# New slots for the steps of an attention and expert kernel on four engine queues

## What is computed

```
# 1: group norm (4 channels a group), attention over all 1024 positions
h = group_norm(x) * gn_scale + gn_bias
w = softmax((h wq + bq)(h wk + bk)^T * 64**-0.5)
x = x + (w (h wv + bv)) wo + bo
# 2: layer norm, causal attention
n = layer_norm(x);  x = x + softmax(causal(n Wq^T (n Wk^T)^T / 8)) (n Wv^T)
# 3: layer norm, experts that choose tokens (32 experts, 8 tokens each, per image)
u = layer_norm(x);  p = softmax(u gate_w^T + gate_b, over the 1024 positions)
topv, topi = the 8 largest of p per image and expert
pooled[b, e] = sum over k of topv * u[topi]
o[b, e] = gelu([pooled, 1] weight1[e]); o = [o, 1] weight2[e]
x = x + scatter_add(topi, topv * o)
```

## Time and profile before

| | |
|---|---|
| median of three runs | 1200.07 us (1199.62 to 1205.99) |
| the profiled execution | 1198.53 us, span 1196.8 us |
| mean granted TensorE clock | 0.845 |
| busy VectorE / ScalarE / GpSimd | 586.5 / 464.6 / 418.9 us |
| DMA | 47.53 MB, mean 40 GB/s |

### The profile page before, as it was taken

One profiled execution on the slowest core, in us unless ns is written; L12 is line 12 of the kernel. 1 busy time (PEld: TensorE's weight loads), 2 busy tenths in 40 slices (PEclk: granted clock), 3 DMA queues, 4 the chain that ended last, 5 costly groups with the idle time before them and its releaser, 6 DMA issues. The chain is left out here.

```text
span 1196.8 us, 14532 instructions
## 1 busy us (share of the span) xinstructions
PE 920.4 (77%) x4278; PEld 527.1 (44%) x4278; DVE 586.5 (49%) x1663; ACT 464.6 (39%) x952; POOL 418.9 (35%) x246
## 2 busy tenths in 40 slices
PE   2777888787888787887878887878878788866546
PEld 1334454534444453535444454545453444434326
DVE  3544554445564554544455544545454545544124
ACT  2222444353535343443435343434435353442320
POOL 1162524262616244242626152442426261610000
PEclk9985978798898888797988888897879888876758
DMA  4010011020201111010202011111102011000089
GB/s 89 11 43 27 18 27 36 5 58 9 58 10 45 23 27 40 27 40 1 57 9 57 9 45 22 26 40 27 31 9 57 9 31 36 23 18 23 18 177 268
DMA packets 67368, 47.53 MB, mean 40 GB/s; under 512 B 36047, under 2 KB 56815, under 8 KB 67311
## 3 DMA queue, kind: packets, MB, share of 16 engines
q1 hardware_dynamic: 67311, 46.90, 16.2%
HBM read 27.88 MB, written 10.49 MB: 32 GB/s over the span
## 5 line engine op out<-in xcount | busy, mean ns | idle before, releaser
L883 ACT ACTIVATE probs<-scores 128x512 f32<-128x512 f32 (+3 forms) x496 | 252.8, 514 | 455.9 <-PE scores L741 450.2
L1121 DVE TENSOR_REDUCE maxima<-maxima_in 128x1 f32<-128x512 f32 (+3 forms) x496 | 276.8, 581 | 271.9 <-PE maxima_in L720 268.0
L970 POOL TENSOR_TENSOR prob_sum<-prob_sum,probs 128x1024 f32<-128x1024 f32 x96 | 227.0, 2365 | 58.4 <-ACT probs L883 54.5
L720 PE MATMUL maxima_in<-keys,queries 128*128 128x512 f32 (+3 forms) x496 | 210.4, 453 | 27.8 <-DVE maxima L1121 27.3
L741 PE MATMUL scores<-queries,keys 128*128 128x512 f32 (+3 forms) x496 | 196.6, 397 | 0.0
L720 PEld LDWEIGHTS maxima_in<-keys,queries 128*128 128x128 f32 x496 | 108.7, 220 | 105.4 <-DVE maxima L1121 72.0
L739 PE MATMUL scores<-queries_lo,keys_hi 65*128 65x512 f32 x256 | 128.4, 502 | 34.2 <-DMA queries_lo<-rows 31.4
L759 PE MATMUL values_out<-probs,x_sb 128*64 128x512 f32 x512 | 144.7, 692 | 1.0 <-ACT probs L883 1.0
L937 POOL TENSOR_TENSOR ln<-ln,minus_half 128x8 f32<-128x8 f32 x32 | 52.8, 1649 | 251.5 <-DVE ln L1106 251.5
L947 POOL TENSOR_TENSOR x_stack<-x_twice,x_stack 64x1024 fp32r<-64x1024 f32 x16 | 37.4, 2339 | 229.9 <-ACT x_stack L819 229.9
L741 PEld LDWEIGHTS scores<-queries,keys 128*128 128x128 f32 x496 | 108.4, 218 | 8.2 <-issue 3.4
(11 more groups left out here) (174 smaller groups left out, 1107.6 us busy)
## 6 DMA issues: line engine op xcount, KB each, us to landing
x_twice<-in_x_t SPq DMA_DIRECT2D x32, 256.0 KB, 4.1
x_halves<-in_x_t SPq DMA_DIRECT2D x16, 256.0 KB, 2.7
x_sb<-in_x SPq DMA_DIRECT2D x16, 256.0 KB, 3.0
keys_hi<-keys SPq DMA_DIRECT2D x16, 256.0 KB, 3.0
u_all<-u_sb SPq DMA_DIRECT2D x16, 256.0 KB, 2.6
t_scratch<-t SPq DMA_DIRECT2D x16, 256.0 KB, 3.0
total<-t_scratch SPq DMA_DIRECT2D x16, 256.0 KB, 4.9
w_sb<-in_w SPq DMA_DIRECT2D x1, 2080.0 KB
```

Source lines behind the costliest of these rows:

```text
L720: pe.matmul(maxima_in[:, p % NM, 0:w * P], queries[s][q][:, c * P:(c + 1) * P], keys[s][q][:, h * HALF:h * HALF + w * P], start=not diagon ...
L883: nc.scalar.activation(probs[:, t % NP, lo:hi], scores[:, (u + (s - 1) * len(UNITS_1)) % NST, 0:hi - lo], ACT.Exp, scale=SCALE).then_inc(e ...
L970: nc.gpsimd.tensor_tensor(prob_sum[:, :], prob_sum[:, :], new, ALU.add).then_inc(rows_added, 1)
L1121: V.reduce_max(maxima[s][:, c, h:h + 1], maxima_in[:, p % NM, 0:w * P], AX.X).then_inc(maxima_taken, 1)
```

## The change

Only the tables of slots change. No instruction is added, removed or altered, and the semaphores keep their order.

```diff
 AT = {
-    "pe": {"f2.out": 2, "p1.qa": 6, "p1.qb": 11, "p1.ka": 16, "p1.kb": 22, "moe.tr": 24, "moe.lg": 26, "r2": 29,
-           "f1.rs": 3, "f1.out": 5, "p1.g1": 7, "p1.g2": 9, "p1.w": 12, "p2.tr": 15, "p2.qa": 19, "p2.qb": 22,
-           "r1": 26},
-    "act": {"p1.qa": 7, "p1.qb": 12, "l2b": 14, "p1.ka": 17, "l2c": 18, "p1.kb": 23, "moe.tr": 25, "moe.lg": 27,
-            "p1.g1": 8, "p1.w": 13, "p2.tr": 15, "p2.qa": 19, "p2.qb": 22, "xp": 24},
-    "dve": {"f2.out": 2, "l2a": 4, "p1.qa": 8, "p1.qb": 13, "p1.ka": 18, "p1.kb": 24, "r2": 28,
-            "p1.st": 1, "f1.rs": 3, "f1.out": 5, "l1a": 6, "p1.g1": 7, "p1.g2": 9, "p1.g3": 11, "p1.w": 13,
-            "p2.tr": 16, "p2.qa": 20, "p2.qb": 23, "r1": 25},
-    "pool": {"l2a": 6, "l1a": 7, "l1b": 8, "p1.g2": 10, "xp": 25},
+    "pe": {"f1.rs": 2, "f1.out": 4, "p1.g1": 1, "p1.g2": 3, "p1.w": 9, "p2.tr": 20, "p2.qa": 27, "p2.qb": 29,
+           "r1": 26, "p1.qa": 6, "p1.qb": 14, "p1.ka": 16, "p1.kb": 22, "r2": 27, "f2.out": 6, "moe.tr": 23,
+           "moe.lg": 24},
+    "act": {"p1.g1": 0, "p1.w": 9, "p2.tr": 20, "p2.qa": 27, "p2.qb": 29, "xp": 22, "p1.qa": 6, "p1.qb": 12,
+            "p1.ka": 16, "p1.kb": 18, "l2b": 17, "l2c": 17, "moe.tr": 18, "moe.lg": 23},
+    "dve": {"p1.st": 0, "f1.rs": 3, "f1.out": 9, "l1a": 9, "p1.g1": 1, "p1.g2": 3, "p1.g3": 6, "p1.w": 10,
+            "p2.tr": 21, "p2.qa": 22, "p2.qb": 29, "r1": 21, "p1.qa": 7, "p1.qb": 14, "p1.ka": 20, "p1.kb": 26,
+            "r2": 29, "f2.out": 0, "l2a": 8},
+    "pool": {"l1a": 20, "l1b": 29, "p1.g2": 11, "xp": 29, "l2a": 17},
 }
 AT_FIRST = {
-    "pe": {"p1.g1": 1, "p1.g2": 2, "p1.w": 4},
+    "pe": {"p1.g1": 1, "p1.g2": 2, "p1.w": 4, "p1.qa": 6, "p1.qb": 11, "p1.ka": 16, "p1.kb": 22},
...
 PIECE_SLOTS = {
-    1: [1, 3, 5, 7, 9, 11, 12, 13, 14, 15, 16, 17, 19, 21, 23],
-    2: [2, 3, 4, 6, 7, 8, 9, 10, 11, 12, 14, 16, 17, 19, 20, 22],
+    1: [7, 7, 11, 15, 17, 17, 18, 19, 21, 21, 23, 23, 24, 24, 26],
+    2: [0, 0, 1, 2, 4, 11, 13, 14, 15, 17, 17, 18, 19, 20, 21, 21],
 }
-VALUE_SLOTS = {1: [9, 17, 25, 1], 2: [9, 17, 24, 1]}
-ADD_SLOTS = [None, 4, 8, 12, 16, 20, 24, 1]
-COPY_SLOT = {1: 2, 2: 2}
-BIAS_SLOT = 6
+VALUE_SLOTS = {1: [15, 27, 28, 1], 2: [10, 22, 29, 0]}
+ADD_SLOTS = [None, 10, 21, 22, 25, 27, 29, 11]
+COPY_SLOT = {1: 0, 2: 1}
+BIAS_SLOT = 12
```

More of the change, by code:

```diff
@@ L63 @@
 AT = {
[9 rows of a table removed]
+    "pe": {"f1.rs": 2, "f1.out": 4, "p1.g1": 1, "p1.g2": 3, "p1.w": 9, "p2.tr": 20, "p2.qa": 27, "p2.qb": 29,
+           "r1": 26, "p1.qa": 6, "p1.qb": 14, "p1.ka": 16, "p1.kb": 22, "r2": 27, "f2.out": 6, "moe.tr": 23,
+           "moe.lg": 24},
[6 rows of a table added]
 }
 AT_FIRST = {
-    "pe": {"p1.g1": 1, "p1.g2": 2, "p1.w": 4},
-    "act": {"p1.g1": 1, "p1.w": 4},
-    "dve": {"p1.st": 0, "p1.g1": 1, "p1.g2": 2, "p1.g3": 3, "p1.w": 4},
[4 rows of a table added]
     "pool": {"p1.g2": 2},
```

## The result

The changed kernel takes 911.9 us (905.89 to 913.72, four runs) where the kernel before took 1202.9 (1199.62 to 1205.99) beside it: a ratio of 0.757, interval 0.753 to 0.762. Its profiled execution took 911.55 us, with a span of 909.8.

The account below looks back on a forecast made before the run. TensorE's waits and the clock falls behind them were taken as the bound: 65.15 = 46.2 + 6.4 + 12.5 us per iteration. Iterations at 49.8 and the edges gain 219 from 1198.5; 979.5, with 1.5 for the median 981 us, range 925 to 1005.

Parts of the forecast that it names:

- ScalarE holds no score: Rival: late exponentials on ScalarE hold TensorE's scores; 52.8 us per iteration, 1023 us in all, chance 0.14.
- f1.rs waits for a sum: Sign of being wrong: second half, f1.rs waits for GpSimd's sums; forecast had them at 2.5 us, f1.rs at 4.0.
- the two with a slow clock: Rivals: clock falls remain in two stretches, 1052 us, chance 0.13; or whole second half at half clock, 1274, 0.08.
- better than 925, with pieces that keep up: Outcome below the forecast range, with VectorE's maxima pieces not delaying TensorE; under 925 us, chance 0.04.
- the clock rival: Rival: short second-half waits still lower TensorE's clock; 54.9 us per iteration, 1052 us in all, chance 0.13.
- 46.2 + 3.65 = 49.8 per iteration: Each loop iteration: TensorE's 46.2 us of work at full clock plus 3.65 of new waits, where it took 65.1.
- p1.ka for p1.qb's low part: First half: TensorE's p1.ka waits 0 to 0.8 us for VectorE's low part of p1.qb, taken as 0.4.
- The row of r2: Second half's first score waits for the row a DMA brings after r2: 0.5 us left of 2.70.
- The pieces: Second half, f1.out to r1: TensorE waits for the piece two before, seven times 0.15 to 0.4, 1.9 us.
- r1: 0.4 taken: End of VectorE's unbroken stretch in the second half: TensorE waits 0.4 us at r1.
- p2.qb: 0.15 taken: Second half: p2.qb waits for p2.qa's copy and subtraction, 0.15 us left of 0.91.
- The 0.8 for the meeting with the bias: First half: VectorE's first l2a addition meets GpSimd's running bias and loses 0.8 us, between nothing and 1.5.

Follow-up runs that it names:

- short_reduce: Changed kernel, but each maxima piece of the second half is reduced over 256 of its 512 columns on VectorE; 894.5 us.
- undo_p1w: Changed kernel with p1.st, p1.g1, p1.g2, p1.g3 and p1.w back at their old slots on TensorE, ScalarE and VectorE; 976.6 us.
- bias_late: Changed kernel with GpSimd's bias addition moved from slot 12 to 18, behind l2a's power; 913.4 us.
- gate_behind: Changed kernel, but in iteration 15's second half VectorE does the first expert gate behind f1.out and l1a, not ahead; 917.0 us.

## Why the prediction was wrong

**The direction and the causes were right.** The waits of f2.out, r2, p1.w and both rows went; the granted clock of an iteration rose from 0.87 to 1.00, and TensorE's busy time fell from 52.63 to 45.55, where 46.2 was expected at full clock. VectorE runs from f1.out to r1 with one pause. ScalarE holds no score, and f1.rs waits for a sum in iteration 15 alone (0.91): those two rivals fell, and so did the two with a slow clock. The time lies where the prediction had put 0.04 ("better than 925, with pieces that keep up"); but the pieces do not quite keep up, by `short_reduce`. Beside the clock rival stood the Trainium skill (TensorE: Matmul & The Clock Gate, "A second HAM failure mode: psum-queue depth-cycling"); the runs bear it out in part. Up to three waits of 0.75 to 1.16 us an iteration left the clock at 1.00 in nearly all iterations; four of 0.90 to 0.97 (`undo_p1w`) brought the lower level in eight of thirteen.

**The step that failed is the sum "46.2 + 3.65 = 49.8 per iteration"; it measures 46.15.** It adds numbers read with two rulers. The 3.65 of new waits came from a walk by starts, in which a matmul of 512 columns takes 0.23 to 0.34 until the next can start. The 46.2 came from busy time, in which the same matmul lasts 0.40 to 0.50, since its modelled end lies behind the next start. After a wait, the first part of the wait lies inside that tail and is called busy. The two pieces at 502.04 take 1.10 us together, 0.40 more than the first pair in `short_reduce`, and only 0.10 of it shows as idle time (each is shown busy for 0.50, and they start 0.60 apart). The second one alone:

```profile
502.64 0.51 PE L722 MATMUL maxima_in<-keys,queries 128*128 128x512 f32 x1
```

So what was added as waits was in part counted as work already. `short_reduce` bounds the true split. Its iteration takes 45.2, and by starts its r1 still waits 0.54 of that (0.65 behind the score at 498.17, for 0.11 between two such scores, 509.71 and 509.82). So TensorE's own work is at most 44.7 and waits are at least 1.45 in the changed kernel. The base was too high by at least 1.5, the waits by the rest of the 3.65, at most 2.2; over 13 iterations 47 us, over the 14th 3.6.

**Its single waits, by starts.** p1.ka for p1.qb's low part: 0.4 taken; p1.ka starts at 476.57, 0.24 behind the matmul ahead, as without a wait: nothing. The row of r2: 0.5 taken; the first score starts 0.24 behind the one ahead too (489.38, 489.62): nothing. The pieces: 1.9 taken, 0.9 to 1.1 found by taking VectorE's work away. r1: 0.4 taken; it starts 0.38 behind the score at 509.82, for 0.11 without a wait: 0.27, up to the negation. p2.qb: 0.15 taken; its operand lands at 512.50, just behind the end of the value group ahead (512.47), and that fits. So the mechanism was right at the pieces, r1 and p2.qb, with sizes too large; two of the waits were not there.

**The lock.** l2a was put at 2.8 us and takes 2.86 (472.82 to 475.68). The 0.8 for the meeting with the bias stood on VectorE's side, with the bias running first; in the trace VectorE's addition starts 0.16 ahead of the bias, and the bias on GpSimd paid 0.45. The addition's 0.75 (0.68 in the earlier trace rows) is not the bias's doing, since it takes 0.76 in `bias_late` too: it starts 0.20 ahead of the end of GpSimd's add (from 470.63 on, 2.39 us). In iteration 15 it starts 0.76 ahead of that end and takes 1.31:

```profile
746.97 2.39 POOL L969 TENSOR_TENSOR prob_sum<-probs 128x1024 f32<-128x1024 f32 x1 [11.73 <-issue]
```

```profile
748.60 1.31 DVE L1095 TENSOR_TENSOR t<-t 128x512 f32<-128x512 f32 x1
```

So the second of the pair to start is the one that is held, as the prediction had it; what it had wrong is which of the two came second. That the pair excludes each other, and that the first to start goes on, agrees with the Trainium skill (SBUF — State Buffer, "SBUF: two separate sides").

**The edges.** Iteration 15's second half was put at nothing, as I took the expert steps for a chain of its own; the turned order on VectorE is most of the 8.4 us there, by `gate_behind`. Its first half gained 8.1 for 5; no run took that apart. Image 0 gained 9.6 for 4. Its 48.8 us become 53.9 in `undo_p1w`, so that about half of the gain is the chain from p1.st to p1.w; the rest stays open. Together: 47 + 3.6 + 11.8 + 5.6 = 68, the difference between 287 and 219.

**What bounds the kernel now** is not what the page says. TensorE is 98% busy in an iteration, yet less work for TensorE, taken behind the last piece, is worth nothing in either half: r1 is released by VectorE, and r2's negation (done at 486.21) lands just ahead of the end of TensorE's cover (486.29). Ahead of the last piece of the first half, and in the second half up to f1.out, VectorE waits for TensorE's pieces; what less work would be worth there no run shows. None of the runs that computes everything beats the changed kernel by more than can be measured.

## What to carry to other kernels

Count one engine's stretch with one ruler: by starts and waits, or by busy and idle time, never a busy time plus waits from a walk by starts. An engine that is busy to the last tenth is shown to be the bound only when taking work from it shortens the time; here the wait came back at the next step that another engine releases. Before a step is moved on an in-order queue, look at all of its parts: the part that waits for another engine (the copy of r1's row, the keys ahead of the row on SP) holds what stands behind it.

## What the runs showed of the hardware

One to three waits of 0.75 to 1.16 us an iteration left the granted clock at full speed in nearly all iterations, even two of them 3.6 us apart; four of 0.90 to 0.97 brought the lower level in eight of thirteen, a wait of 1.79 in eight of fourteen, and one of 3.97 made a value group take 3.53 us for 1.94. What decides, and why the same 1.16 stood at the lower level in the kernel before, these runs do not settle; there a wait of 1.92 lay ahead of it.

A GpSimd addition that started 0.16 us behind a VectorE addition of the same size, both reading SBUF, took 1.73 us for 1.28. A VectorE addition that started 0.76 us ahead of the end of a running GpSimd addition took 1.31 for 0.68.
